# Cross-attention and mixture-of-experts block: the start-up ("filling") of the attention pipeline rearranged

## The chip, the core and the metric

The kernel runs on one core of a Trainium2 chip. The metric is the device time of one execution in microseconds (us); lower is better. The engines are TensorE (PE in the profile, its weight loads PEld), VectorE (DVE), ScalarE (ACT), GpSimd (POOL) and SyncE (SP, which here only issues transfers). They run side by side and wait for each other on semaphores.

## The reference, cut to what matters

```python
# x (2,1024,256), ctx (2,154,256); 16 heads of 16; 8 experts, 2 chosen per token, hidden 1024
def attention(query, ctx):                        # _L0_xattn_ref
    q = einsum('bsd,hdk->bhsk', query, Wq) + bq   # queries
    k = einsum('bsd,hdk->bhsk', ctx, Wk) + bk     # keys
    v = einsum('bsd,hdk->bhsk', ctx, Wv) + bv     # values, with their bias
    attn = softmax(einsum('bhqk,bhsk->bhqs', q, k) / sqrt(16))
    return concat_heads(attn @ v) @ Wo + bo
x = x + attention(layernorm(x), ctx)
x = x + experts(layernorm(x))                     # router, top 2 of 8, gelu MLP, weighted sum
```

## The kernel before, in words

The 2048 tokens are worked on in 8 pairs of tiles (m = 0 to 7, 256 tokens each; four pairs per batch entry). For each pair the kernel normalises x (`norm1`), turns it (`xn_transposes`), makes the queries (`q_product`, evacuated by `evac_q`) and splits them into a high and a low part (`evac_q` on ScalarE, `low_queries` on GpSimd), so that fp32 accuracy comes out of fast products. The two parts must then be spread over partitions into the tile `QS` (rows 0 to 31 high, 32 to 63 low, 64 to 95 high again, 96 to 99 the negated maxima). For pair 0 the engines copy them there on chip (`first_queries` on ScalarE, line 707, the loop at line 948 on VectorE, `first_low_queries` on GpSimd, line 519). For all other pairs SP stores them to the DRAM tensor `qd` (`queries`, line 376), and GpSimd's queue reads them back into `QS` (`queries_read`, lines 505 and 506). `by_memory(m)` says how many such round trips the slot of pair m has seen; the ring has four slots.

With `QS` and the keys `KS`, `scores(m, n)` (line 1477, n = 0 to 7) makes the scores of a pair into one of two buffers of PSUM, VectorE takes their maxima (`maxima`, line 1001), negates and splits them (`negatives`), TensorE turns them (`maxima_transposes`, line 1492), ScalarE evacuates them (`evac_maxima`, line 675), SP stores them and GpSimd's queue reads them into rows 96 to 99 of `QS` (`maxima_read`, line 511). Then `turned_scores(m, n)` (lines 1523 and 1526, n = 0 to 9) makes the scores again, keys on partitions, less the maxima; ScalarE takes their exponentials (`exp`, line 684), and `value_sums` (lines 1549 and 1551) multiplies them by the values.

The order on each engine is written out by hand; each engine carries out its list strictly in that order. First stands a filling, in which pairs 0 and 1 pass their scores; then step m (0 to 7) interleaves `scores` of pair m+2, `turned_scores` of pair m, and `value_sums` and the output projection of pair m-1. Step 0 begins with `scores(2, 0)`. After the attention come the routing and the expert products (lines 1826, 1843, 1846), where TensorE is busy nearly all the time.

The values are made once, in the filling: `value_product(b)` (lines 1451 and 1455) for b = 0 and 1, one after the other, before `scores(0, 0)`. VectorE adds the bias while it places them (`values`, lines 981 and 987) and writes the column of ones (`all_values`, line 993); both stand in VectorE's list between pair 0's and pair 1's maxima. In the same stretch ScalarE's list has `ones` (line 713, the selector rows of `KS`), `last_keys` (line 726), `evac_q`, `evac_xnT` and `evac_maxima`. TensorE's list there is: `value_product(0)`, `value_product(1)`, `scores(0, 0..7)` with pair 2's transposes and query product among them, `maxima_transposes(0)`, `scores(1, 0..7)` with pair 3's, `maxima_transposes(1)`, and then step 0.

Of the kernel before, what the change touches and what calls it, by code (L numbers as in the profile page):

```python
# [7 lines left out]
B, S, D = 2, 1024, 256  # L8
# [26 lines left out]
def xattn_moe_kernel(nc, x, ctxT, wq, bq, wk, bk, wv, bv, wo, bo, rwT, wexp,  # L35
# [11 lines left out]
    with ExitStack() as ctx:  # L47
# [196 lines left out]
        q0_high, q0_mid, q0_low = sem("q0_high"), sem("q0_mid"), sem("q0_low")  # L244
        ld_x2, ld_id, ld_bq = sem("ld_x2"), sem("ld_id"), sem("ld_bq")
        v_psum, v_made = sem("v_psum"), sem("v_made")
# [44 lines left out]
        def by_memory(m):  # L291

            return m // RING + int(m % RING > 0)
# [58 lines left out]
        def _(sp):  # L352
# [46 lines left out]
            queries(1)  # L399
# [30 lines left out]
        def _(pool):  # L430
# [51 lines left out]
            def low_queries(m):  # L482
                u = m % 2
                pool.wait_ge(q_hi_made, m + 1)
                if m >= 3:
                    pool.wait_ge(qd_stored[(m - 2) % RING], 64 * by_memory(m - 2))
                pool.tensor_tensor(Q2[:, u, 1, :, :].bitcast(f32r), qf[:, :, :], Q2[:, u, 0, :, :],
                                   ALU.subtract).then_inc(q_lo_made, 1)
# [24 lines left out]
            def first_low_queries():  # L513

                low_queries(0)
                for r in range(4):
                    pool.wait_ge(*((q0_low, r) if r else (q_lo_made, 1)))
                    pool.tensor_copy(QS[32:64, 0, 2 * r:2 * r + 2, :], Q2[32 * r:32 * r + 32, 0, 1, :, :]).then_inc(q0_low, 1)
                pool.wait_ge(q0_low, 4)  # L520
# [111 lines left out]
        def _(act):  # L632
# [23 lines left out]
            def evac_q(m):  # L656
                act.wait_ge(q_psum, m + 1)
                if m >= 1:
                    act.wait_ge(q_lo_made, m)
                for g in range(GROUPS):  # L660
# [3 lines left out]
                if m == 2:  # L664
                    act.wait_ge(q0_low, 4)
                if m >= 3:
# [37 lines left out]
            def first_queries():  # L704

                for r in range(4):
                    act.activation(QS[0:32, 0, 2 * r:2 * r + 2, :], qf[32 * r:32 * r + 32, :, :], ACT.Copy).then_inc(q0_high, 1)
# [30 lines left out]
            first_queries()  # L738
# [171 lines left out]
        def _(dve):  # L910
# [66 lines left out]

            def values(b):
                dve.wait_ge(v_psum, b + 1)
                bank = ps_v[b]  # L980
                dve.tensor_tensor(V_main[:, b, :, 0:DK], bank[:, 0:D].rearrange("p (h c) -> p h c", h=HEADS),
                                  bv_sb[:, :].rearrange("p (h c) -> p h c", h=HEADS), ALU.add).then_inc(v_made, 1)
                for j in range(4):
                    lanes = slice(32 * j, 32 * j + REM)
                    rest = bank[lanes, D:2 * D].rearrange("p (q j c) -> p q j c", j=4, c=DK)
                    bvr = bv_sb[lanes, :].rearrange("p (q j c) -> p q j c", j=4, c=DK)
                    dve.tensor_tensor(V_rest[lanes, b, :, 32 * j:32 * j + DK], rest[:, :, j, :], bvr[:, :, j, :],
                                      ALU.add).then_inc(v_made, 1)
            def all_values():
                dve.wait_ge(ld_v, 32)  # L990
                dve.wait_ge(v_zeroed, 2)
                for j in range(4):
                    dve.memset(V_rest[32 * j:32 * j + REM, :, :, 32 * j + DK:32 * j + DK + 1], 1.0).then_inc(v_made, 1)
                for b in range(B):
                    values(b)
# [64 lines left out]
            all_values()  # L1060
# [352 lines left out]
        def _(pe):  # L1413
# [35 lines left out]
            def value_product(b):  # L1449
                for c in range(KC):  # L1450
                    mm(ps_v[b][:, 0:D], ctx_sb[:, c, b * KEYS:b * KEYS + P], wv_sb[:, c, :],
                       start=c == 0, stop=c == KC - 1)
                for c in range(KC):
                    for j in range(4):
                        last = mm(ps_v[b][32 * j:32 * j + REM, D:2 * D],
                                  ctx_sb[:, c, b * KEYS + P:(b + 1) * KEYS], wv_sb[:, c, :],
                                  start=c == 0, stop=c == KC - 1)
                last.then_inc(v_psum, 1)

            def scores(m, n):  # L1460

                i, k, u, b = n // 4, n % 4, m % RING, m // (MACROS // B)
                if n == 0:
                    if by_memory(m):
                        pe.wait_ge(qs_loaded[u], 32 * by_memory(m))
                    else:
                        for made in (q0_high, q0_mid, q0_low):
                            pe.wait_ge(made, 4)
                        pe.wait_ge(k_made, 2)
# [29 lines left out]
            def turned_scores(m, n):  # L1499
# [5 lines left out]
                if n == 0:  # L1505
# [3 lines left out]
                    if m == 0:  # L1509
                        pe.wait_ge(v_made, 4 + 5 * B)  # L1510
# [137 lines left out]
            for b in range(B):  # L1648
                value_product(b)
# [78 lines left out]
            def step(m, has):  # L1728
                if m >= QUIET:
                    quiet_step(m)  # L1730
                    return
                if has(2):
# [7 lines left out]
                if has(0):  # L1740
# [12 lines left out]
                if has(0):  # L1753
                    turned_scores(m, 1)
# [162 lines left out]
```

## Time and profile before

| | us |
|---|---|
| Runs of the kernel before | 454.33, 457.53, 464.33 (median 457.53) |
| The profiled execution's own time | 454.56 |
| Its span | 452.6 |
| TensorE busy in the span | 397.0 (88%) |
| VectorE, ScalarE, GpSimd busy | 275.9, 228.6, 201.6 |
| Mean granted TensorE clock | 0.95 of full |

The profile is one execution. Its time is the span and 1.96 us around it. Starts are counted from the start of the span. A line of the timeline merges instructions of one kind that follow each other, so its length can hold short waits, and neighbouring matmul lines overlap by the pipeline. The granted clock is 1.00 (2.4 GHz) or 0.50 (1.2 GHz); a value between is a stretch with both.

### The profile page before, as it was taken

How to read it: one execution, taken by the hardware profiler on the slowest of the kernel's cores; microseconds unless marked ns; L12 is line 12 of the kernel's file. 1: busy time of each engine (PE TensorE's matmuls, PEld its weight loads, DVE VectorE, ACT ScalarE, POOL GpSimd, SP SyncE). 2: the span in 40 equal slices, each digit the busy share in tenths (PEclk: the TensorE clock that was granted, in tenths of full speed). 3: DMA queues.
4: the chain of work that ended last, by engine and by line, in shares of the span. 5: the costliest groups of instructions: out<-in, count | busy, mean ns of one | idle time of the engine just before them, and what ended most of it. 6: DMA issues, size and time to landing. Idle time of an engine off the chain costs nothing.

```text
span 452.6 us, 8677 instructions
## 1 busy us (share of the span) xinstructions
PE 397.0 (88%) x2742; PEld 332.7 (74%) x2743; DVE 275.9 (61%) x655; ACT 228.6 (51%) x420; POOL 201.6 (45%) x183
## 2 busy tenths in 40 slices
PE   6766798999999998658899999999999999999920
PEld 3445666768667675626899999999999999999910
DVE  2989748456476757787857556454466867464300
ACT  1843647456455654332674655544567766544300
POOL 4947567372623322005153644535445544452230
PEclk9986998999999999859999999999999999999985
DMA  7455552433610111754636435343252662332220
GB/s 240 133 116 123 122 121 76 97 98 73 169 42 13 54 49 47 234 187 126 247 68 180 82 105 143 58 129 47 47 139 47 220 151 38 55 49 25 25 28 12
DMA packets 25750, 45.39 MB, mean 100 GB/s; under 512 B 6512, under 2 KB 19952, under 8 KB 22960
## 3 DMA queue, kind: packets, MB, share of 16 engines
q0 software_dynamic: 8448, 15.77, 19.4%
q1 hardware_dynamic: 13760, 26.32, 18.2%
q10 hardware_dynamic: 3504, 2.83, 2.1%
q8 instruction: 20, 0.33, 0.3%
q14 instruction: 18, 0.15, 0.1%
HBM read 31.52 MB, written 13.39 MB: 99 GB/s over the span
## 4 chain that ended last, share of the span: by engine, by line
PE 73%; DVE 11%; DMA 4%; issue 3%; ACT 2%; POOL 1%; SPq 0%; ACTq 0%; DVEq 0%; POOLq 0%
PE ps_s L1826 23%; PE ps_t L1843 15%; PE ps_t L1846 8%; PE ps_s L1477 3%; DVE mx L1001 2%; PE ps_t L1526 2%; PE ps_a L1551 2%; PE ps_a L1549 2%; DMA result<-big,rowtok 2%; PE ps_c L1551 2%; PE ps_c L1808 2%; PE ps_t L1523 2%; PE ps_c L1549 2%; PE ps_t L1420 2%; PE ps_a L1577 1%
## 5 line engine op out<-in xcount | busy, mean ns | idle before, releaser
L1826 PE MATMUL ps_s<-xgT,KB 128*128 128x256 f32 x912 | 115.4, 282 | 3.0 <-DVE xgT L1358 3.0
L622 POOL DMA_INDIRECT result<-big,rowtok x38 | 66.8, 1759 | 112.3 <-DMA result<-big,rowtok 54.8
L1826 PEld LDWEIGHTS ps_s<-xgT,KB 128*128 128x128 f32 x912 | 110.1, 189 | 4.1 <-DVE xgT L1358 1.7
L1001 DVE TENSOR_REDUCE mx<-ps_s 128x4 f32<-128x616 f32 x64 | 49.3, 797 | 31.1 <-PE ps_s L1477 31.0
L590 POOL DMA_INDIRECT big<-rows,gtok x38 | 43.3, 1140 | 31.9 <-DVE gtok L1315 14.7
L1843 PE MATMUL ps_t<-KB,HTb 128*128 x160 | 56.0, 392 | 0.0
L684 ACT ACTIVATE big<-ps_t 128x512 f32<-128x512 f32 x80 | 45.2, 593 | 20.7 <-PE ps_t L1526 18.0
L876 ACT ACTIVATE big<-ps_t,wrow 128x256 f32<-128x256 f32 x38 | 18.0, 474 | 70.1 <-PE ps_t L1846 70.1
L1843 PE MATMUL ps_t<-KB 128*128 x144 | 50.4, 392 | 0.0
L1404 DVE SCALAR_TENSOR_TENSOR big<-ps_t,wrow,big 128x256 f32<-128x256 f32 x38 | 18.4, 483 | 52.5 <-ACT big L876 49.2
L868 ACT ACTIVATE big<-ps_s 128x512 f32<-128x512 f32 x76 | 45.5, 599 | 0.0
L1846 PE MATMUL ps_t<-KB,HTb 128*128 x160 | 44.7, 280 | 0.0
L1477 PE MATMUL ps_s<-KB 96*128 96x308 f32 x128 | 33.7, 357 | 7.6 <-DVE mx L1001 3.6
L1846 PE MATMUL ps_t<-KB 128*128 x144 | 40.3, 280 | 0.0
L452 POOL TENSOR_TENSOR mv<-mv,half_sb 128x2 f32<-128x2 f32 x15 | 10.9, 728 | 59.7 <-DVE mv L1045 42.6
L1843 PEld LDWEIGHTS ps_t<-KB,HTb 128*128 128x128 f32 x160 | 30.0, 188 | 6.3
L1374 DVE TENSOR_TENSOR KB<-big,KB 128x512 fp32r<-128x512 f32 x36 | 24.4, 691 | 16.1 <-ACT big L868 16.1
L866 ACT ACTIVATE HTb<-ps_s 128x512 fp32r<-128x512 f32 x40 | 24.0, 600 | 20.1 <-PE ps_s L1826 17.6
L1374 DVE TENSOR_TENSOR HTb<-big,HTb 128x512 fp32r<-128x512 f32 x40 | 26.6, 689 | 11.0 <-ACT big L868 11.0
L1526 PE MATMUL ps_t<-KB 100*128 100x256 f32 x128 | 29.3, 325 | 4.2 <-ACT big L684 3.9
L1477 PEld LDWEIGHTS ps_s<-KB 96*128 96x128 f32 x128 | 21.4, 208 | 13.7 <-DVE mx L1001 6.9
L1843 PEld LDWEIGHTS ps_t<-KB 128*128 128x128 f32 x144 | 27.0, 187 | 5.6
(234 smaller groups left out, 710.3 us busy)
## 6 DMA issues: line engine op xcount, KB each, us to landing
VP<-in_wexp SPq DMA_DIRECT2D x8, 1024.0 KB, 5.3
big<-in_wexp SPq DMA_DIRECT2D x8, 1024.0 KB, 5.5
qd<-big SPq DMA_DIRECT2D x28, 128.0 KB, 2.3
KB<-qd POOLq DMA_DIRECT2D x7, 512.0 KB, 5.3
result<-x SPq DMA_DIRECT2D x8, 256.0 KB, 2.7
rows<-xn SPq DMA_DIRECT2D x8, 256.0 KB, 2.9
KB<-qd POOLq DMA_DIRECT2D x7, 256.0 KB, 6.0
XS<-in_x ACTq DMA_DIRECT2D x1, 1024.0 KB, 5.8
```

What stands on the lines that cost most here:

```text
L590: pool.indirect_dma_start(XG[:, n, :], None, rows, bass.IndirectOffsetOnAxis(gtok[:, n:n + 1], 0)).then_inc(xg_loaded[u % 2], 16)
L622: pool.indirect_dma_start(out, bass.IndirectOffsetOnAxis(rowtok[:, u, h:h + 1], 0), ys[:, 2 * (u % 2) + h, :], None, compute_op=ALU.add).t ...
L684: act.activation(dst, ps_t[(n + 1) % 2][:, :].rearrange("p (h n) -> p h n", h=2), ACT.Exp).then_inc(p_made, 1)
L866: act.activation(hidT[u % 2][:, 0, 2 * b:2 * b + 2, :], ps_s[b // 2][:, b % 2, :].rearrange("p (j n) -> p j n", j=2), ACT.Gelu)
L868: act.activation(hid[:, b, :], ps_s[b // 2][:, b % 2, :], ACT.Gelu).then_inc(hid_made, 1)
L1001: dve.tensor_reduce(mx[:, i, :, 2 * k:2 * k + 2].rearrange("p a b -> p b a"), ps_s[n % 2][:, :, 0:2 * KEYS].rearrange("p b (h k) -> p b h ...
L1374: dve.tensor_tensor(hidT[u % 2][:, 1, js, :], hid[:, b, :].rearrange("p (j n) -> p j n", j=2), hidT[u % 2][:, 0, js, :].bitcast(fp32), ALU ...
L1477: last = mm(ps_s[n % 2][:, j, 0:2 * KEYS], QS[0:96, u, p, i * P:(i + 1) * P], KS[0:96, b, p, :], start=True, stop=True)
L1526: last = mm(bank[:, h, :], KS[0:100, b, place(j - 2), h * KEYS:h * KEYS + P], QS[0:100, u, place(j - 2), :], start=True, stop=True)
L1826: last = mm(ps_s[j // 4][:, j // 2 % 2, (j % 2) * PAIR:(j % 2 + 1) * PAIR], w1[:, w, k, j * P:(j + 1) * P], xgT[:, u % 2, a, k, :], start= ...
L1843: mm(ps_t[h][:, :].rearrange("p (w d) -> p w d", w=2), hidT[u % 2][:, 0, j, half_rows], w2[:, bass.ds(par, 1), :, j, :].squeeze(1), start= ...
L1846: last = mm(ps_t[h][:, 0:D], hidT[u % 2][:, 1, j, half_rows], w2[:, bass.ds(par, 1), 0, j, :].squeeze(1), start=False, stop=j == HJ - 1, s ...
```

## The change

Four things are changed, all in the filling and at the head of step 0.

1. The bias of the values is added by TensorE: one more product (identity by the bias rows) for each main and each remainder group. ScalarE copies the result into place. VectorE keeps only the four small writes of ones, now before its copies of pair 0's queries.
2. Pair 1's queries are no longer stored and read back. ScalarE copies the high part twice (`first_queries(1)`, `queries_again`), GpSimd the low part (`first_low_queries(1)`). The counts of round trips change with it.
3. `value_product(1)` stands behind `scores(0, 7)`, ahead of `maxima_transposes(0)`. On ScalarE, `ones(0)` now stands whole behind `evac_q(2)`, `last_keys(0)` behind `evac_maxima(0)`, and then both `values`. GpSimd's queue takes `maxima_read(0)` ahead of `queries_read(2)`.
4. In step 0 `turned_scores(0, 0)` and `(0, 1)` stand first, ahead of `scores(2, 0)`.

```diff
         def by_memory(m):
-            return m // RING + int(m % RING > 0)
+            return m // RING + int(m % RING > 1)
@@ sync
-            queries(1)
             queries(2)
             maxima(0)
@@ gpsimd
             def low_queries(m):
-                if m >= 3:
+                if m >= 4:
                     pool.wait_ge(qd_stored[(m - 2) % RING], 64 * by_memory(m - 2))
-            first_low_queries()
+            first_low_queries(0)
             middle_keys(0)
-            low_queries(1)
-            queries_read(1)
+            first_low_queries(1)
             low_queries(2)
             next_norm1(3)
+            maxima_read(0)
             queries_read(2)
-            maxima_read(0)
             next_norm1(4)
@@ scalar
+            def queries_again():
+                for r in range(4):
+                    act.activation(QS[64:96, 1, 2 * r:2 * r + 2, :], qf[32 * r:32 * r + 32, :, :], ACT.Copy).then_inc(q1_mid, 1)
+
+            def values(b):
+                act.wait_ge(v_psum, b + 1)
+                act.wait_ge(v_zeroed, 2)
+                bank = ps_v[b]
+                act.activation(V_main[:, b, :, 0:DK], bank[:, 0:D].rearrange("p (h c) -> p h c", h=HEADS),
+                               ACT.Copy).then_inc(v_made, 1)
+                for j in range(4):
+                    lanes = slice(32 * j, 32 * j + REM)
+                    rest = bank[lanes, D:2 * D].rearrange("p (q j c) -> p q j c", j=4, c=DK)
+                    act.activation(V_rest[lanes, b, :, 32 * j:32 * j + DK], rest[:, :, j, :], ACT.Copy).then_inc(v_made, 1)
...
-            first_queries()
+            first_queries(0)
...
             evac_q(1)
-            ones(0, (0,))
+            first_queries(1)
             evac_xnT(2)
-            ones(0, (1,))
+            queries_again()
+            evac_q(2)
+            ones(0)
+            evac_maxima(0)
             last_keys(0)
-            evac_q(2)
-            evac_maxima(0)
+            values(0)
+            values(1)
             evac_xnT(3)
@@ vector
+            dve.wait_ge(v_zeroed, 2)
+            for j in range(4):
+                dve.memset(V_rest[32 * j:32 * j + REM, :, :, 32 * j + DK:32 * j + DK + 1], 1.0).then_inc(v_ones, 1)
             dve.wait_ge(qf_made, 1)
...
             statistics1(3)
-            all_values()
@@ tensor, value_product(b)
+                mm(ps_v[b][:, 0:D], id_sb[:, :], bv_sb[:, :], start=False, stop=True)
...
+                for j in range(4):
+                    last = mm(ps_v[b][32 * j:32 * j + REM, D:2 * D], id_sb[:, 32 * j:32 * j + REM], bv_sb[:, :],
+                              start=False, stop=True)
@@ tensor, filling
-            for b in range(B):
-                value_product(b)
+            value_product(0)
...
             for n in range(4 + GROUPS, 8):
                 scores(0, n)
+            value_product(1)
             maxima_transposes(0)
@@ tensor, step(m, has)
+                if m == 0:
+                    turned_scores(0, 0)
+                    turned_scores(0, 1)
                 if has(2):
                     scores(m + 2, 0)
```

The waits are changed to match: `scores(1, 0)` waits for the copies instead of the read, and `turned_scores(0, 0)` for ten placed values and the four writes of ones.

## Rows read from the trace of the kernel before

**Rows 1.** Busy time by stage: PE, PEld, DVE, ACT, POOL, granted clock, DMA.

```profile
330.00:370.00 40.00, 40.00 (x286) 37.52 (x286) 27.84 (x56) 25.09 (x45) 19.00 (x15) 1.00 0.55 151
```

**Rows 2.** The chain that ended last, 43 to 60 us: start, length, what.

```profile
43.83 0.88 PE ps_c L1444 x4
...
48.98 2.22 DMA qd<-big
...
52.13 5.66 DMA KB<-qd
...
57.83 0.55 PE ps_s L1477 x2
```

**Rows 3.** TensorE's timeline of the filling: start, length, line, operation.

```profile
18.15 1.03 PE L1451 MATMUL ps_t<-big 128*128 128x256 f32 x4
...
20.10 1.13 PE L1451 MATMUL ps_t<-big 128*128 128x256 f32 x4
...
31.12 0.55 PE L1477 MATMUL ps_s<-KB 96*128 96x308 f32 x2 [0.60 <-DVE mx L1001]
33.20 0.40 PE L1492 MATMUL ps_a<-id_sb,nm 128*32 128x128 f32 x2 [1.53 <-DVE nm L1014]
35.47 1.40 PE L1477 MATMUL ps_s<-KB 96*128 96x308 f32 x4 [1.88 <-DMA KB<-qd]
...
45.16 0.40 PE L1492 MATMUL ps_a<-id_sb,nm 128*32 128x128 f32 x2 [0.47 <-DVE nm L1014]
45.31 0.82 PE L1477 MATMUL ps_s<-KB 96*128 96x308 f32 x4
45.97 0.65 PE L1523 MATMUL ps_t<-KB 100*128 100x256 f32 x4
...
51.48 1.89 PE L1444 MATMUL ps_c<-xnT,wq_sb 128*128 128x256 f32 x8
...
57.03 0.38 PE L1492 MATMUL ps_c<-id_sb,nm 128*32 128x128 f32 x2
```

**Rows 4.** VectorE's timeline of the filling.

```profile
22.98 2.03 DVE L1054 TENSOR_SCALAR xn<-XS,mv 128x256 f32<-128x256 f32 x2
...
34.17 0.47 DVE L993 MEMSET VP<- 26x8 f32 x4
...
37.34 1.51 DVE L1001 TENSOR_REDUCE mx<-ps_s 128x4 f32<-128x616 f32 x2
...
45.89 2.25 DVE L1001 TENSOR_REDUCE mx<-ps_s 128x4 f32<-128x616 f32 x3 [0.78 <-PE ps_s L1477]
```

**Rows 5.** ScalarE's timeline of the filling.

```profile
13.00 2.57 ACT L707 ACTIVATE KB<-qf 32x512 fp32r<-32x512 f32 x4
...
28.18 0.84 ACT L726 ACTIVATE KB<-KB 100x104 fp32r<-100x104 f32 x4
29.98 0.84 ACT L661 ACTIVATE qf<-ps_a,bq_sb 128x256 f32<-128x256 f32 x2 [0.97 <-PE ps_a L1444]
...
41.29 2.34 ACT L713 ACTIVATE KB<-own 4x1232 fp32r<-4x1232 f32 x2
```

**Rows 6.** GpSimd's timeline of the filling.

```profile
17.07 2.87 POOL L519 CAST KB<-big 32x512 fp32r<-32x512 f32 x4
...
23.59 1.27 POOL L487 TENSOR_TENSOR big<-qf,big 128x512 fp32r<-128x512 f32 x1
...
35.13 2.44 POOL L463 TENSOR_SCALAR xn<-XS,mv 128x256 f32<-128x256 f32 x2
...
38.22 0.53 POOL L506 DMA_DIRECT2D KB<-qd  x1
```

**Rows 7.** Stages at low granted clock, columns as in the first group.

```profile
24.60:28.20 3.60, 3.13 (x11) 2.79 (x12) 3.29 (x5) 1.84 (x3) 0.26 (x1) 0.55 0.54 135
...
35.10:42.00 6.90, 5.21 (x18) 4.46 (x19) 6.32 (x19) 1.31 (x2) 4.19 (x6) 0.51 0.72 159
76.10:79.40 3.30, 3.28 (x15) 1.73 (x16) 1.72 (x6) 0.80 (x2) 2.16 (x3) 0.51 0.68 199
```

More of the change, by code:

```diff
@@ L511, in maxima_read, with first_low_queries @@
                 pool.dma_start(QS[96:100, u, :, :], md[u, :, :].rearrange("(r q) n -> r q n", q=PAIRED)).then_inc(nm_loaded[u], 16)
-            def first_low_queries():
-                low_queries(0)
+            def first_low_queries(m):
+                low_queries(m)
                 for r in range(4):
-                    pool.wait_ge(*((q0_low, r) if r else (q_lo_made, 1)))
-                    pool.tensor_copy(QS[32:64, 0, 2 * r:2 * r + 2, :], Q2[32 * r:32 * r + 32, 0, 1, :, :]).then_inc(q0_low, 1)
-                pool.wait_ge(q0_low, 4)
+                    pool.wait_ge(*((q0_low, 4 * m + r) if r else (q_lo_made, m + 1)))
+                    pool.tensor_copy(QS[32:64, m, 2 * r:2 * r + 2, :], Q2[32 * r:32 * r + 32, m, 1, :, :]).then_inc(q0_low, 1)
+                pool.wait_ge(q0_low, 4 * m + 4)
             def middle_keys(b):
@@ L659, in evac_q @@
                     act.wait_ge(q_lo_made, m)
+                if m == 2:
+                    act.wait_ge(q0_high, 8)
+                    act.wait_ge(q1_mid, 4)
                 for g in range(GROUPS):
@@ L663, in evac_q @@
                 last.then_inc(qf_made, 1)
-                if m == 2:
-                    act.wait_ge(q0_low, 4)
-                if m >= 3:
+                if m in (2, 3):
+                    act.wait_ge(q0_low, 4 * m - 4)
+                if m >= 4:
                     act.wait_ge(qd_stored[(m - 2) % RING], 64 * by_memory(m - 2))
@@ L976, in low_keys @@
                                     KM[b][32 * r:32 * r + 32, 1, :, :, :].rearrange("p g a k -> p (g a k)")).then_inc(ks_low, 1)
[L978 to L993, printed above, removed]
-                for b in range(B):
-                    values(b)
             def maxima(m, n):
@@ L1451, in value_product @@
                     mm(ps_v[b][:, 0:D], ctx_sb[:, c, b * KEYS:b * KEYS + P], wv_sb[:, c, :],
-                       start=c == 0, stop=c == KC - 1)
+                       start=c == 0, stop=False)
+                mm(ps_v[b][:, 0:D], id_sb[:, :], bv_sb[:, :], start=False, stop=True)
                 for c in range(KC):
                     for j in range(4):
-                        last = mm(ps_v[b][32 * j:32 * j + REM, D:2 * D],
-                                  ctx_sb[:, c, b * KEYS + P:(b + 1) * KEYS], wv_sb[:, c, :],
-                                  start=c == 0, stop=c == KC - 1)
+                        mm(ps_v[b][32 * j:32 * j + REM, D:2 * D],
+                           ctx_sb[:, c, b * KEYS + P:(b + 1) * KEYS], wv_sb[:, c, :],
+                           start=c == 0, stop=False)
+                for j in range(4):
+                    last = mm(ps_v[b][32 * j:32 * j + REM, D:2 * D], id_sb[:, 32 * j:32 * j + REM], bv_sb[:, :],
+                              start=False, stop=True)
                 last.then_inc(v_psum, 1)
@@ L1466, in scores @@
                     else:
-                        for made in (q0_high, q0_mid, q0_low):
-                            pe.wait_ge(made, 4)
-                        pe.wait_ge(k_made, 2)
+                        for made in (q0_high, q0_low):
+                            pe.wait_ge(made, 4 * m + 4)
+                        pe.wait_ge((q0_mid, q1_mid)[m], 4)
+                        if m == 0:
+                            pe.wait_ge(k_made, 2)
                     if m % (MACROS // B) == 0:
@@ L1509, in turned_scores @@
                     if m == 0:
-                        pe.wait_ge(v_made, 4 + 5 * B)
+                        pe.wait_ge(v_made, 5 * B)
+                        pe.wait_ge(v_ones, 4)
                     if m >= 1:
@@ L1647, in _ @@
             pe.wait_ge(ld_v, 32)
-            for b in range(B):
-                value_product(b)
+            value_product(0)
             for n in range(2):
@@ L1731, in step @@
                     return
+                if m == 0:
+                    turned_scores(0, 0)
+                    turned_scores(0, 1)
                 if has(2):
@@ L1739, in step @@
                     value_sums(m - 1, 1)
-                if has(0):
+                if has(0) and m:
                     turned_scores(m, 0)
@@ L1753, in step @@
                 if has(0):
-                    turned_scores(m, 1)
+                    if m:
+                        turned_scores(m, 1)
                     turned_scores(m, 2)
```

8 lines of the change are left out of this document (4 added, 4 removed).

## The prediction

> **What bounds the kernel now.** I read the busy time by stage first: from the expert stage on TensorE is busy for all of a 40 us window [rows 1], and nothing of the change is there. What the filling gains or loses can therefore only arrive as a shift of everything behind it. So I read the chain of waits next, to see what sets the start of step 1, the first stretch in which TensorE's list runs without waits. It is pair 3's queries: from the second half of their product at 43.83 by way of ScalarE, GpSimd, SP's four stores (the last lands 2.22 later) and the read back (5.66) to `scores(3, 0)` at 57.83, 14.0 in all [rows 2]. But that chain wins narrowly. TensorE's own list ends step 0 with `maxima_transposes(2)` at 57.03 [rows 3]; the same pair of lines follows at 0.15 distance elsewhere (45.16, 45.31, rows 3), so without the read `scores(3, 0)` would start at 57.2. A faster chain alone is worth 57.83 - 57.2 = 0.6; more has to come from an earlier step 0. There VectorE's maxima set the pace: they start at 45.89 [rows 4], and pair 4's query product waits behind them until 51.48 [rows 3].
>
> **The change part by part.** I walk the lists with the durations of the trace; a small "+" is against before.
>
> *Start, VectorE.* The four writes of ones take 0.47 to 0.50 with the gaps [rows 4]. They stood between pair 0's and pair 1's maxima and now stand ahead of a stretch in which VectorE never rests, so pair 2's normalised x, finished at 25.01 [rows 4], comes 0.5 later. Its transposes and product follow. Part of their work moves past 28.2, where the granted clock rises from half (0.55 on average until then, rows 7) to full, so I count +0.4 from there on. `ks_low` also comes 0.5 later (23.45) and stays just inside GpSimd's copies; `scores(0, 0)` does not move.
>
> *Pair 1's queries.* ScalarE: four copies take 2.57 [rows 5], twice. The first set ends at 22.8 + 2.6 = 25.4, before pair 2's transposes at 26.7; the second ends at 29.9, before pair 2's product at 30.4. Nobody waits for ScalarE. GpSimd: `low_queries(1)` ends at 24.86 and the copies take 2.87 [rows 6], to 27.7; its next work needs pair 2's queries at 31.9. So all of pair 1 is in place by 29.9, where the read let `scores(1, 0)` start at 35.47 [rows 3]. SP loses four stores, GpSimd's queue two reads.
>
> *Values on TensorE.* One `value_product` takes 20.10 - 18.15 = 1.95 [rows 3]. The bias is one more product for each two, so 2.9 with it. `value_product(0)` ends at 21.2 instead of two at 22.2: hidden, `scores(0, 0)` waits until 23.76 for keys. `value_product(1)` now starts behind `scores(0, 7)`, 31.67 [rows 3] + 0.4 less overlap = 32.0, ends at 34.9, and holds back `maxima_transposes(0)`, which was at 33.20 [rows 3]: +1.7. Behind it `scores(1, 0)` starts at 35.1 against 35.47: the read that is saved is nearly all spent on this product.
>
> *VectorE freed.* Before, `maxima(1, 0)` waited for VectorE, which was placing values until 37.34 [rows 4]. Now VectorE takes it 0.55 behind the scores, at 35.65. Four maxima (3.0), `statistics1(4)` (1.2), four maxima (3.0) follow, to 42.7; before to 44.67. Negatives and a hand-over are 0.5: `maxima_transposes(1)` at 43.2 against 45.16 [rows 3], -2.0.
>
> *Values on ScalarE.* `evac_maxima(0)` at 35.3 to 35.7; `last_keys` 0.84 [rows 5]; then ten placements. None is in the trace on ScalarE. By the nearest rows a wide one is 128x256, 0.42 (half of 0.84), a small one between 0.2 and 0.28 (a 100x104 copy, both rows 5): 1.2 to 1.5 for each b; I take 1.25 because the small ones are 64 columns. All end at 39.05, then `evac_xnT(3)` to 39.7 (turned by 38.5, so this is now 0.5 to 0.6 late), `ones(1)` 2.34 [rows 5] to 42.0. TensorE makes the two halves of pair 3's product at 39.75 and, behind `scores(1, 7)`, at 41.7 to 42.6. The head of the chain at 43.83 becomes 41.7, and its end 57.79 becomes 55.6: -2.2. GpSimd is not in its way: `norm1(4)` ends at 43.1, ScalarE delivers at 44.15.
>
> *GpSimd's queue.* GpSimd ends `norm1(3)` (2.44, rows 6) at 38.0; the maxima are stored by 35.75 + 2.0 = 37.75. `maxima_read(0)` costs 0.53 of issue ahead of `queries_read(2)`, whose second read then goes out at 39.2 instead of 38.22 [rows 6] and lands 5.66 later [rows 2] at 44.9. Before, it was there at 43.9 and held nobody; now `scores(2, 0)` waits for it. The two turned scores put ahead (0.65 and 0.3, rows 3) fit into 43.4 to 44.7, so they cost nothing here, and are cover for the read. The maxima are there by 43.7 at the latest. `scores(2, 0)` at 44.9 against 45.31, -0.4; VectorE's maxima follow with the same -0.4, and with them pair 4's product, its queries and the last five exponentials.
>
> *Step 1.* TensorE: 57.2 - 0.4 = 56.8. The read: 55.6, no longer late. `scores(3, 0)` at 56.8 instead of 57.83.
>
> **The sum:** -1.0. Of the 2.2 that the chain gains, 1.2 are not used, since step 0's own list is next in line. The profiled execution took 454.56, so 453.5. Its own time lies 3 us under the median of the three runs (457.53) and at their lowest, which I take up in the range.
>
> **One cover that may be thin.** Pair 2's second normalisation is slow: both take 2.03 [rows 4], while GpSimd's subtraction runs beside it [rows 6]. Behind that subtraction now stand four copies of 0.72 where GpSimd was idle. If one of them gets in first, pair 2 comes another 0.7 later, the read's landing moves from 44.9 to 45.6, step 1 to 57.5, and the gain shrinks to 0.3: 454.2. The Trainium skill ("SBUF — State Buffer", "Who interferes with whom") says that a VectorE instruction in a two-port mode and a GpSimd one exclude each other for the whole instruction, and that order of issue decides. The slow row agrees; by this rule one or two such losses are to be expected, and the sum would be 454.2 instead of 453.5. I keep 453.5, because the two normalisations now start before the copies do.
>
> **The rivals.**
> *Slower: `value_product(1)` at half clock.* The granted clock came back at 28.2 after a stretch in which TensorE was busy 3.13 of 3.60 [rows 7]. The stretch now starts 0.5 later after a longer pause (from 21.2, not 22.2). If it comes back only with the next busy stretch, pair 2's product and the scores beside it lose about 1.5, and the product of 2.9 can cost 5.8. Then `maxima_transposes(0)` stands at 34.9 + 1.5 + 2.9 = 39.3, its maxima are stored at 42.1, `queries_read(2)` lands at 49.0, VectorE starts at 49.6, 3.7 late, and step 1 at 60.9: 457.7. It decides from the point where `maxima_transposes(0)` starts later than 36.3 (from there the read lands so late that step 1 is back at 57.8). For it: the lower clock did hit 6.9 us in a row from 35.1 [rows 7]. Against it: from 25.6 on work is dense. With half clock for the scores only it gives 454.7. Chance 0.2.
> *More gain: the whole chain.* If the read lands with time to spare (there are two reads less on the queue, and the maxima go first) and step 0 shortens too, all of 2.2 is gained: 452.4. Against it: the reads took the same time alone, and turned scores hold TensorE until 44.7, so -0.6 is the most that step 0 can give by this list. Chance 0.05.
> *The dip moves.* From 76.1 to 79.4 TensorE was granted half clock while busy for 3.28 [rows 7]; half of that, 1.6, is lost. The clock does not follow my shift exactly; the dip may vanish (451.9) or a second one come (455.1). The half clock from 35.1 to 42.0 should go, since `value_product(1)` fills the pause before it, but VectorE sets the pace there. Chance 0.15.
> *The change doesn't do what it says*: the values placed by ScalarE turn out so slow (over 0.6 for a small one) that pair 3's transposes wait and the chain is back at 57.8: 454.6 or a little more. Chance 0.05.
>
> **How the numbers follow.** The forecast (453 to 454.6 with the thin cover inside) has 0.55. The likeliest time is 453.5. The low end is the vanished dip with the largest gain, 452.4 - 1.6, rounded to 450.5. The high end is the half-clock rival, 457.7, with the distance of about 1.5 by which a median may lie over a single execution: 459. A difference of 2% (9.1 us) is about what a measurement of this kernel can tell from no change; no case comes near it on either side. Only the spread of the runs (454.33 to 464.33) could bring it about: faster 0.03, slower 0.03, within 0.94.
>
> **What would show it.** In the profile after: `value_product(1)` between 32.0 and 34.9; the first maxima of pair 1 at 35.7 instead of 37.34; ScalarE's ten placements in 2.5; no wait for a read before `scores(3, 0)`, but one before `scores(2, 0)`, near 44.9; the granted clock full from 35 to 42; step 1 at 56.8. It would be wrong if `maxima_transposes(0)` starts after 36.3, if `scores(2, 0)` comes later than 45.9, or if `scores(3, 0)` still ends a wait for its read.

## The result and the profile after

The changed kernel takes 458.98 us (median of 20 runs, 454.43 to 467.0), the kernel before 455.36 (20 runs, 452.25 to 464.33). Their ratio is 1.0064, with a 95% interval of 1.0039 to 1.0089: 0.64% or 2.9 us slower, where 1.0 less was forecast. The ratio leaves out runs more than 1.5% above the fastest of their kernel, so it is not that of the two medians; the execution that was profiled, 461.63, is such a run, and I therefore read from its trace where time went, and take no size from its total.

Two rows of the page of the changed kernel, the span and the granted clock in 40 slices:

```profile
span 459.8 us, 8726 instructions
...
PEclk9889799999999999669999999999999998999975
```

**The filling did nearly what was forecast up to 47 us.** TensorE's timeline of the changed kernel (start, length, line, operation, wait ahead of it); it answers to [rows 3]:

```profile
32.23 1.03 PE L1454 MATMUL ps_t<-big 128*128 128x256 f32 x4
...
34.50 0.61 PE L1464 MATMUL ps_t<-bv_sb,id_sb 128*26 128x256 f32 x8
35.05 0.39 PE L1502 MATMUL ps_a<-id_sb,nm 128*32 128x128 f32 x2
35.20 0.82 PE L1487 MATMUL ps_s<-KB 96*128 96x308 f32 x4
...
43.26 0.39 PE L1502 MATMUL ps_a<-id_sb,nm 128*32 128x128 f32 x2 [0.58 <-DVE nm L1018]
...
45.50 0.83 PE L1487 MATMUL ps_s<-KB 96*128 96x308 f32 x4 [1.05 <-DMA KB<-qd]
...
52.03 2.92 PE L1447 MATMUL ps_c<-xnT,wq_sb 128*128 128x256 f32 x8
...
58.62 0.38 PE L1502 MATMUL ps_c<-id_sb,nm 128*32 128x128 f32 x2
58.76 0.53 PE L1487 MATMUL ps_s<-KB 96*128 96x308 f32 x2
```

`value_product(1)` stands behind `scores(0, 7)`, `scores(1, 0)` waits for no read, the second turned maxima come 1.9 earlier than before (43.26 against 45.16), and a read is now waited for at `scores(2, 0)`. Then pair 4's query product takes 2.92 instead of 1.89 [rows 3], and step 1 starts at 58.76, 0.93 later than before.

The other engines of the changed kernel, VectorE's timeline (it answers to [rows 4]), ScalarE's [rows 5] and GpSimd's [rows 6]:

```profile
22.95 2.03 DVE L1058 TENSOR_SCALAR xn<-XS,mv 128x256 f32<-128x256 f32 x2
...
35.77 2.96 DVE L1005 TENSOR_REDUCE mx<-ps_s 128x4 f32<-128x616 f32 x4 [0.74 <-PE ps_s L1487]
```

```profile
36.61 0.36 ACT L719 ACTIVATE VP<-ps_t 128x256 f32<-128x256 f32 x1
36.88 0.92 ACT L724 ACTIVATE VP<-ps_t 26x64 f32<-26x64 f32 x4
37.82 0.38 ACT L719 ACTIVATE VP<-ps_t 128x256 f32<-128x256 f32 x1
38.10 0.92 ACT L724 ACTIVATE VP<-ps_t 26x64 f32<-26x64 f32 x4
```

```profile
24.89 2.61 POOL L518 CAST KB<-big 32x512 fp32r<-32x512 f32 x4
...
35.89 2.43 POOL L462 TENSOR_SCALAR xn<-XS,mv 128x256 f32<-128x256 f32 x2
38.60 0.81 POOL L510 DMA_DIRECT2D KB<-md  x1 [0.27 <-DMA md<-nmT]
```

The clock took back what was won. Busy time by stage of the changed kernel, columns as in [rows 1], and the expert stage's window under it:

```profile
35.00:47.00 12.00, 8.24 (x47) 5.75 (x43) 8.27 (x18) 8.96 (x24) 9.50 (x10) 1.00 0.51 117
47.00:55.00 8.00, 7.92 (x30) 7.04 (x31) 6.86 (x15) 2.29 (x5) 5.29 (x7) 0.57 0.74 160
...
76.00:79.40 3.40, 3.08 (x26) 1.40 (x25) 2.20 (x8) 1.69 (x4) 1.69 (x2) 1.00 0.69 189
330.00:370.00 40.00, 40.00 (x283) 37.38 (x282) 29.19 (x58) 25.86 (x46) 18.33 (x12) 1.00 0.52 144
```

The half clock of 35.1 to 42.0 and that of 76.1 to 79.4 [rows 7] are gone; a new stretch at 0.57 lies at 47 to 55, where TensorE is busy for 7.92 of 8.

**The time was lost in the expert stage.** Its first product starts at 209.61 before and at 208.49 after, 1.1 earlier; TensorE's last product ends at 432.66 and 440.96, 8.3 later. The expert stage grew from 223.05 to 232.47. Two pauses of TensorE, 2.52 and 4.88, are 7.4 of these 9.4, both for the rows that GpSimd gathers for one of the later experts; before has no such pause. Most of the rest is a stretch of 3.4 at half clock that begins at 378.4, as the second pause ends. TensorE's timeline, first the kernel before, then the changed one:

```profile
276.74 2.04 PE L1826 MATMUL ps_s<-xgT,KB 128*128 128x256 f32 x16
278.61 0.60 PE L1808 MATMUL ps_c<-id_sb,big 128*128 128x128 f32 x4
```

```profile
280.27 0.66 PE L1823 MATMUL ps_c<-id_sb,big 128*128 128x128 f32 x4 [2.52 <-DMA big<-rows,gtok]
...
378.68 1.12 PE L1823 MATMUL ps_c<-id_sb,big 128*128 128x128 f32 x4 [4.88 <-DMA big<-rows,gtok]
```

The window of [rows 1] lies between the two: it is as full as before, and shows nothing.

### The profile page after: what moved, and what is told of

The parts are those of the page before. It is cut to its first block, busy times and chain, and to the rows that moved or that the text cites. A ratio compares the mean times of both kernels' runs of the same rounds, so it can differ in the third digit from the quotient of the medians.

```text
span 459.8 us, 8726 instructions
## 1 busy us (share of the span) xinstructions
PE 402.5 (88%) x2762; PEld 336.7 (73%) x2763; DVE 274.0 (60%) x645; ACT 235.5 (51%) x438; POOL 208.0 (45%) x185
## 4 chain that ended last, share of the span: by engine, by line
PE 59%; DMA 12%; DVE 11%; issue 5%; ACT 4%; POOL 2%; DVEq 0%; ACTq 0%; POOLq 0%
PE ps_s L1841 17%; PE ps_t L1858 10%; DMA result<-big,rowtok 7%; PE ps_t L1861 5%; PE ps_s L1487 3%; PE ps_t L1537 3%; DMA big<-rows,gtok 3%; DVE mx L1005 2%; PE ps_a L1562 2%; PE ps_c L1562 2%; PE ps_a L1560 2%; PE ps_t L1534 2%; PE ps_c L1560 2%; PE ps_c L1823 1%; PE ps_t L1423 1%
## 5 line engine op out<-in xcount | busy, mean ns | idle before, releaser
L620 POOL DMA_INDIRECT result<-big,rowtok x38 | 69.9, 1840 | 115.7 <-DMA result<-big,rowtok 70.8
L588 POOL DMA_INDIRECT big<-rows,gtok x38 | 45.2, 1190 | 31.7 <-DVE gtok L1318 14.9
L1407 DVE SCALAR_TENSOR_TENSOR big<-ps_t,wrow,big 128x256 f32<-128x256 f32 x38 | 18.4, 483 | 55.0 <-ACT big L896 54.5
L1858 PEld LDWEIGHTS ps_t<-KB,HTb 128*128 128x128 f32 x160 | 30.0, 188 | 6.3
L1861 PEld LDWEIGHTS ps_t<-KB,HTb 128*128 128x128 f32 x160 | 30.1, 188 | 0.0
```

The source lines that it names most:

```text
L588: pool.indirect_dma_start(XG[:, n, :], None, rows, bass.IndirectOffsetOnAxis(gtok[:, n:n + 1], 0)).then_inc(xg_loaded[u % 2], 16)
L620: pool.indirect_dma_start(out, bass.IndirectOffsetOnAxis(rowtok[:, u, h:h + 1], 0), ys[:, 2 * (u % 2) + h, :], None, compute_op=ALU.add).t ...
L1858: mm(ps_t[h][:, :].rearrange("p (w d) -> p w d", w=2), hidT[u % 2][:, 0, j, half_rows], w2[:, bass.ds(par, 1), :, j, :].squeeze(1), start= ...
L1861: last = mm(ps_t[h][:, 0:D], hidT[u % 2][:, 1, j, half_rows], w2[:, bass.ds(par, 1), 0, j, :].squeeze(1), start=False, stop=j == HJ - 1, s ...
```

## The experiments

All intervals are 95% intervals of the ratio to the kernel before. The expert stage is measured in each trace from its first product to TensorE's last.

The expectations name their theories by letters. A: the loss sits in the expert stage, carried by GpSimd's queue of gathers and adds. B: it sits in the filling. Later, I: the position of TensorE's instructions in its list makes the pause. R: rounding of the values sends tokens to other experts.

**Which part does it?** Three kernels undo one part each, and the changed kernel runs again beside them.

Turned scores back behind `scores(2, ...)`:

```diff
-                if m == 0:
-                    turned_scores(0, 0)
-                    turned_scores(0, 1)
...
-                if has(0) and m:
+                if has(0):
...
-                    if m:
-                        turned_scores(m, 1)
+                    turned_scores(m, 1)
```

> The changed kernel with part 4 undone: scores(2, 0) again first in step 0, turned_scores(0, 0) and (0, 1) in their old places. Theory B (late read, then half clock in step 0): the turned scores no longer fill the wait, so step 0 is longer by up to 1 and the first expert product moves to 209 or later. Theory A: the attention may move by less than 1 and the total stays near 1.006 of before, since no transfer changes.

Measured: 0.9986 (0.9919 to 1.0053); expert stage 225.99, with a pause of 2.43.

Pair 1's queries by memory again (the waits and `by_memory` are changed back with it):

```diff
+            queries(1)
             queries(2)
...
-            first_low_queries(1)
+            low_queries(1)
+            queries_read(1)
...
-            first_queries(1)
             evac_xnT(2)
-            queries_again()
```

> The changed kernel with part 2 undone: pair 1's queries go by memory again (four stores, two reads on GpSimd's queue), with the other parts in place. Theory A, with GpSimd's queue as the carrier: the number of transfers that this queue has taken before the expert stage is that of before again, so the expert stage is back near 223 and the total near 1.000, though the attention is later by 1 to 3, as value_product(1) now delays pair 1 and the read is late too. Theory B: the filling is slower still, total 1.01 or more.

Measured: 1.0043 (1.0001 to 1.0085); expert stage 225.95, with a pause of 2.73. Neither theory's forecast for the trace came: the queue's transfers are those of before again, yet the pause is there, so their number is not the cause; and the filling is not slower in the trace, where the first expert product comes at 206.96, earlier than in any other here.

Bias and placing of the values back on VectorE, both value products first (the small products for the bias are gone from TensorE):

```diff
-            value_product(0)
+            for b in range(B):
+                value_product(b)
...
-            value_product(1)
...
             statistics1(3)
+            all_values()
...
-            values(0)
-            values(1)
```

> The changed kernel with parts 1 and 3's place of value_product(1) undone: VectorE adds the bias and places the values, both products stand before scores(0, 0); pair 1's queries copied on chip and the turned scores first stay. By the walk of the prediction maxima_transposes(0) is back at 33.2, scores(1, 0) follows at once, but VectorE is busy with the values until 37.3 as before: the attention within 1 of before. Theory A: total still near 1.005, since the queue's transfers are those of the changed kernel. Theory B: the half clock in step 0 goes, total 0.997 to 1.000.

Measured: 1.0016 (0.9983 to 1.0049); expert stage 223.12, no pause, though the queue's transfers are those of the changed kernel.

The changed kernel again:

> The changed kernel, unchanged, for a second profile and a second comparison. In the first profile the attention was ahead (the first expert product at 208.5 against 209.6) and the expert stage longer (from that product to TensorE's end 232.5 against 223.1, with two waits for gathered rows of 2.5 and 4.9). Theory A, the loss sits in the expert stage, where GpSimd's one queue carries gathers and adds: first expert product again near 208.5, expert stage at least 225, ratio near 1.006. Theory B, the loss sits in the filling (the read of pair 2's queries comes late and TensorE drops to half clock in step 0) and the first profile was a lucky one there: first expert product at 211 or later, expert stage near 223.

Measured: 0.9991 (0.9955 to 1.0026); expert stage 225.79, with a pause of 2.50 at 276.9. The first expert product comes at 207.66, not at 211 or later, so B's forecast failed. A's stage came, its ratio near 1.006 did not. Of the two pauses the first came back, in `u_turned` and `u_queries` too; the second, 4.88, did not. Only the kernel whose values stay on VectorE is without it. Two reasons remain. The one, routing: the values' bias is rounded otherwise when TensorE adds it, so tokens could go to other experts. The other, position: the ten bias products in 32-bit floats are forty instructions (each is two products and two weight loads in the trace), with the waits that the change adds some 42; the whole list of TensorE behind them moves by as much.

**Position or routing?** The kernel before, with 21 tiny products (42 instructions) put in at its start:

```diff
             keep_busy(17)
+            for _ in range(21):
+                mm(ps_t[0][:, 0:32], ones_bf[:, :], ones_bf[:, 0:32], start=True, stop=True)
```

> The kernel before with 21 products of 32 columns behind the warming ones at the start, in a pause of TensorE: 42 more instructions of TensorE, as many as the change adds (20 matmuls, 20 weight loads, 2 waits), and nothing else changed. Theory I: the instruction packet moves from 54.5 to 52.5, between the packets of the adds, the wait of 2.5 comes, the expert stage is 225.8, ratio 1.005 to 1.007. Theory R (the bias added in another place rounds the values otherwise, and other tokens go to the experts): values are those of before, so expert stage 223.1, ratio 1.000.

Measured: 1.0029 (0.9984 to 1.0074); expert stage 225.84, with a pause of 2.51 at 282.2. Nothing of the change is in it, its values are those of before, and the pause is there. The ratio is under the 1.005 to 1.007 that was expected.

The same 21 products in the changed kernel:

> The changed kernel with the same 21 small products. Theory I: the instruction packet moves on by another 2 to 3, to about 50, where no packets of gathers or adds are; the expert stage is back near 223 and the total is the gain of the attention alone, ratio 0.996 to 0.998. Theory R: nothing moves, expert stage 225.8, ratio as the changed kernel.

Measured: 1.0002 (0.996 to 1.0044); expert stage 224.73, a pause of 1.13. A miss for theory I: the pause is shorter but not gone, and the packet did not move on to 50; it lies at 53.0, where the changed kernel without the 21 products has it too (52.7 to 52.9).

The changed kernel with 40 instructions less: the runs of empty products that are meant to keep the clock up (`keep_busy`), at the start and ahead of the expert stage, are made of fewer and longer ones.

```diff
+            def keep_busy_fp32(n):
+                for _ in range(n):
+                    mm(ps_t[0][:, :].rearrange("p (a n) -> p a n", a=4), zero[:, 0:P],
+                       zero[:, 0:P].unsqueeze(1).to_broadcast([P, 4, P]), start=True, stop=True)
...
-            keep_busy(17)
+            pe.wait_ge(zero_made, 1)
+            keep_busy_fp32(4)
...
-            keep_busy(20)
+            keep_busy_fp32(4)
+            keep_busy(1)
```

> The changed kernel with its 37 warming products of bf16 (512 columns) replaced by 8 of fp32 on a tile of zeros and 1 of bf16, about as long together, with 40 instructions fewer: TensorE's instruction count ahead of the expert stage is that of before plus a few. Theory I: the packet is back at 54.5, the expert stage 223.1, the total 0.996 to 0.998 of before. Theory R: expert stage 225.8.

Measured: 0.9988 (0.9948 to 1.0027); expert stage 223.25, no pause, with the values of the change. Routing is refuted from both sides: a pause with the old values, none with the new.

The kernel before again:

> The kernel before, unchanged, for its second profile. So far every trace with the values' bias on TensorE (four of four) has a wait of 2.4 to 2.7 for gathered rows 69 us into the expert stage, and neither of the two with the values on VectorE has it (the kernel before, u_values). Theory I (position of TensorE's instructions): no such wait here, expert stage 223.1 from the first expert product to TensorE's end, one 16 KB packet of the instruction queue between 54.5 and 55 us into it, ratio 1.000. If it were chance: the wait can be here too, near 226.

Measured: 1.0027 (0.9992 to 1.0062); expert stage 223.08, no pause. A kernel against itself gives 1.0027: single comparisons differ by that much.

One of them comes 52.5 to 54.5 us after the first expert product. DMA by queue, in windows of 2 us at the same place behind that product (52 to 54, and 54 to 56 where a second follows); columns: packets, MB, share of 16 engines. Before, changed kernel, before with 21 products, changed kernel with 40 instructions less:

```profile
q0 software_dynamic: 210, 0.33, 72.0%
q1 hardware_dynamic: 38, 0.18, 21.8%
...
q0 software_dynamic: 30, 0.07, 9.4%
q8 instruction: 1, 0.02, 2.9%
```

```profile
q0 software_dynamic: 205, 0.33, 68.1%
q1 hardware_dynamic: 38, 0.18, 22.5%
q8 instruction: 1, 0.02, 2.9%
```

```profile
q0 software_dynamic: 196, 0.31, 66.9%
q1 hardware_dynamic: 45, 0.24, 29.2%
q8 instruction: 1, 0.02, 2.9%
```

```profile
q0 software_dynamic: 204, 0.32, 68.2%
q1 hardware_dynamic: 46, 0.25, 29.6%
...
q0 software_dynamic: 36, 0.07, 10.3%
q8 instruction: 1, 0.02, 2.9%
```

In the second and third the packet lies among the dense packets of queue 0, GpSimd's gathers and its add; in the first and last it comes when these are nearly through. Its place goes with the count, but not in step. 16 products and as many weight loads take 2.04 in the expert stage (276.74, above), so 42 instructions are, as an estimate, 2.7 us of TensorE's list; from before to `b_pad21` the packet moves by 1.7 (54.6 to 52.9), from the changed kernel to `a_pad21` not at all, though the next one there moves from 69.4 to 65.5. The Trainium skill ("Runtime: NRT & Kernel Launch", "Instruction fetch mechanics") says that an engine's list is fetched in blocks of 16 KiB, and that crossing a block is mostly hidden. The 16 KB packets agree. Whether TensorE itself waits for a block no run here tests; if the reading below is right, this one had a cost all the same, by way of the gathers. What follows is in GpSimd's timeline, same order of kernels:

```profile
264.63 1.63 POOL L622 DMA_INDIRECT result<-big,rowtok  x1 [2.70 <-DMA result<-big,rowtok]
...
271.54 1.02 POOL L590 DMA_INDIRECT big<-rows,gtok  x1 [0.30 <-issue]
272.86 1.19 POOL L590 DMA_INDIRECT big<-rows,gtok  x1 [0.30 <-issue]
```

```profile
264.29 1.63 POOL L620 DMA_INDIRECT result<-big,rowtok  x1 [3.38 <-DMA result<-big,rowtok]
...
272.76 1.46 POOL L588 DMA_INDIRECT big<-rows,gtok  x1 [0.30 <-issue]
```

```profile
268.76 1.63 POOL L622 DMA_INDIRECT result<-big,rowtok  x1 [3.42 <-DMA result<-big,rowtok]
...
277.22 1.46 POOL L590 DMA_INDIRECT big<-rows,gtok  x1 [0.31 <-issue]
```

```profile
264.54 1.63 POOL L620 DMA_INDIRECT result<-big,rowtok  x1 [2.46 <-DMA result<-big,rowtok]
...
272.38 1.23 POOL L588 DMA_INDIRECT big<-rows,gtok  x1 [0.30 <-issue]
```

The add ahead of these gathers waits 3.4 for an earlier one to land, instead of 2.5 to 2.7. So the next two gathers are issued 0.7 and 1.0 later after the first expert product, and the second one ends its issue behind an issue of SP that it otherwise beats, the 1 MB load of the next expert's weights. SP's own list, before and changed kernel:

```profile
274.43 0.33 SPq L392 DMA_DIRECT2D VP<-in_wexp  x1
```

```profile
273.40 0.33 SPq L392 DMA_DIRECT2D VP<-in_wexp  x1
```

Before, the second gather ends at 272.86 + 1.19 = 274.05, ahead of 274.43; changed, at 272.76 + 1.46 = 274.22, behind 273.40. Its rows then land too late, and TensorE waits 2.5. The order holds in all 18 traces of this text: the nine without a pause have the gather's end ahead of the load, the nine with one behind it. Where the landing is on record, the gather lands 3.0 to 3.1 after its start without the pause (5 traces) and 7.4 to 7.7 after it with it (3). Two things stay open. No kernel here moves the load alone. And `a_pad21` has the long wait of the add (3.43) and the turned order, but a pause of 1.13 only; its next instruction packet lies at 65.5 instead of 69.4, which may be the reason and was not tested.

**Is it repeatable, and what is the change worth without it?** The changed kernel and the one with 40 instructions less again, and two further edits on the latter. First the repeats:

> The changed kernel a third time, beside the same with 40 instructions fewer (next). Theory I (position of TensorE's instructions): expert stage 225.8 or more with the wait of 2.5 near 69 us into it, instruction packet at 52.5; from the end of pair 2's normalisation to the first expert product 183.4 (182.5 to 184.6 in the four traces with this order); ratio 1.003 (attention -1.2, expert stage +2.7). Theory R (rounding) expects the same here.

Measured: 1.0009 (0.9963 to 1.0054); expert stage 227.16, with a pause of 2.48 and, as it ends, a stretch of 3.4 at half clock.

> The changed kernel with the 37 warming products replaced by 9, 40 instructions fewer, a second time. Theory I: expert stage 223.2, packet at 54.5, ratio 0.997, and 2 to 3 us below a_third in the same job. Theory R: as a_third.

Measured: 0.9977 (0.9945 to 1.0009); expert stage 223.10, no pause.

Pair 2's queries read ahead of the maxima, on the shortened kernel (the changed kernel with 40 instructions less):

```diff
-            maxima_read(0)
             queries_read(2)
+            maxima_read(0)
```

> The version with 40 instructions fewer, and GpSimd's queue takes queries_read(2) ahead of maxima_read(0) as before the change. By the walk the read of pair 2's queries then lands 0.7 to 0.9 earlier (44.7 instead of 45.5 in the trace after), scores(2, 0) no longer waits 1.05 but at most 0.3, and the maxima land by 44.5 and may hold turned_scores(0, 0) by up to 1. If the late read is what costs step 0 its time: attention 0.5 to 0.8 shorter, ratio 0.996. If the one transfer only swaps places with the other: attention as a_short2.

Measured: 1.0003 (0.9965 to 1.004). A miss: TensorE now waits 1.75 at 44.8 for the maxima, and later 1.71 and 1.15, as its timeline shows:

```profile
46.59 0.74 PE L1539 MATMUL ps_t<-KB 100*128 100x256 f32 x4 [1.75 <-DMA KB<-md]
...
55.33 0.88 PE L1492 MATMUL ps_s<-KB 96*128 96x308 f32 x2 [1.71 <-DVE mx L1005]
```

Nothing here speaks for the old order of the two reads.

Both value products first, on the shortened kernel:

```diff
-            value_product(0)
+            for b in range(B):
+                value_product(b)
...
-            value_product(1)
```

> The version with 40 instructions fewer, and value_product(1) again directly behind value_product(0). By the walk scores(0, 0) starts 0.4 later (the two products end at 24.1), maxima_transposes(0) at 33.9 and scores(1, 0) at 34.1 instead of 35.1, so pair 1's maxima are 1.0 earlier, and the maxima of pair 0 are stored 1.0 earlier, though GpSimd's norm1(3) sets when they are read: attention 0.3 to 0.8 shorter. Against it: TensorE has a pause between 32.2 and 33.9 again, and half clock may follow it as in the kernel before (35.1 to 42.0); VectorE sets the pace there, so it costs at most 0.5.

Measured: 0.9963 (0.9927 to 0.9999); expert stage 223.09, no pause.

Then each of the four main kernels once more:

> The kernel before with 21 small products at the start, again. Theory I (position of TensorE's instructions): packet at 52.5, expert stage 225.8, ratio 1.004 to 1.007. If the packet's place costs only in some executions, the trace can have it and the ratio is within 0.003 of 1.

Measured: 1.0031 (0.9997 to 1.0065), again under what was expected; expert stage 227.45, pause 2.61, and half clock for 3.4 as it ends.

> The changed kernel, a fourth time. Theory I: packet at 52.5, expert stage 225.8 or more, ratio 1.001 to 1.005 (the three so far: 1.0064, 0.9991, 1.0009), above a_short3 by 0.004 to 0.006.

Measured: 0.9978 (0.9927 to 1.0028); expert stage 226.00, pause 2.71.

> The changed kernel with 40 instructions fewer ahead of the expert stage, a third time. Theory I: packet at 54.5, expert stage 223.1 to 223.3, ratio 0.997 to 0.999 (so far 0.9988, 0.9977).

Measured: 0.996 (0.9928 to 0.9993); expert stage 223.05, no pause.

> The same with value_product(1) again directly behind value_product(0), a second time. The first gave 0.9963 (0.9927 to 0.9999), its trace an attention no shorter than that of a_short2 (183.6 from the end of pair 2's normalisation to the first expert product in both) and an expert stage of 223.1. If the place of value_product(1) gains something, ratio below 0.998 again; if not, it is that of a_short3 within 0.003.

Measured: 0.9972 (0.9934 to 1.001); expert stage 223.21, no pause.

**Taken together.** 18 traces fall into groups by where the instruction packet lies behind the first expert product (read in steps of 0.5 us):

| packet at | kernels | traces | expert stage | pause |
|---|---|---|---|---|
| 53.5 to 54.5 | before twice, `u_values`, `a_short` three times, `s_reads`, `s_vfirst` twice | 9 | 223.05 to 223.25 | none |
| 53.0 | `a_pad21` | 1 | 224.73 | 1.13 |
| 52.5 | changed four times, `u_turned`, `u_queries`, `b_pad21` twice | 8 | 225.79 to 232.47 | 2.43 to 2.73 |

So with the packet at 52.5 the pause costs 2.7 in the trace (225.8 - 223.1), whatever else is in the kernel, and 4.1 and 4.4 in the two traces where half clock follows it (227.16 and 227.45).

In times it is harder to see. Four comparisons of the changed kernel gave 1.0064, 0.9991, 1.0009 and 0.9978; they lie further apart than their intervals allow. Their plain mean is 1.0011, weighted by their intervals 1.0028. The shortened kernel's three (0.9988, 0.9977, 0.996) have means of 0.9975 and 0.9973. The shortening is thus worth 0.0036 to 0.0055, 1.6 to 2.5 us, not far from 2.7. The padded kernel before does not bear it out: it gave 1.0029 and 1.0031, where 2.7 us would be 1.006, and the kernel before, unchanged, gave 1.0027 beside it. So what the pause costs over many executions is not settled. That the changed kernel is slower than before by 2.9 holds for the first comparison; over all four it is 0.5 to 1.3 us slower, and the difference is not settled. The shortened changed kernel comes out 1.2 us faster than before (weighted 0.9973, half interval 0.0020). All three comparisons point that way, but one of a kernel with itself was off by as much (1.0027), so this is likely and not shown.

## Why the prediction was wrong

**The step that failed** is one of its first sentences: that nothing of the change is in the expert stage, so that the filling can only arrive as a shift. [rows 1] showed a stage in which TensorE is always busy, and it was still busy in that window after. But the list that TensorE reads there lies 42 instructions further on, and 2.7 us were lost at another place of the stage, most likely since a packet that fetches the list fell among GpSimd's gathers. I counted the bias products by their duration (about 0.95 of `value_product`'s 2.9) and not by their length in the list. `b_pad21` shows that the length alone brings the pause. The shift that was forecast, 1.0, did arrive (1.1); with 2.7 against it the trace would be 1.6 slower. The first comparison gave 2.9, the mean of four 0.5 to 1.3.

**The second pause** of the profiled execution (4.88 at 373.8) is in none of the seventeen other traces. It follows an add at 362.07 whose issue took 3.69 instead of 1.6. It is a cause of that execution's 461.63, and its own cause stays open.

**The filling, step by step.** Held: `value_product(1)` 32.23 to 35.1 (forecast 32.0 to 34.9); pair 1's maxima from 35.77 (35.65); the ten placements in 2.4 (2.5), a wide one 0.36, four small ones 0.92; `maxima_transposes(1)` at 43.26 (43.2); the wait moved from the read for `scores(3, 0)` to that for `scores(2, 0)`, at 45.50 (44.9); full clock from 35 to 42. Off by 0.5: pair 2's normalised x was to come 0.5 later and ended at 24.98 against 25.01, since the 0.47 of the writes were won back ahead of it (VectorE's four casts took 2.17 instead of 2.31, its masks 1.02 instead of 1.35). The thin cover was not tested: the rule of the Trainium skill ("SBUF — State Buffer", "Who interferes with whom") would have let GpSimd's copies delay that normalisation, but they started at 24.89, as it ended.

**Step 1 at 56.8** failed: 58.76. By 45.5 the list was 0.6 behind the forecast: GpSimd ended `norm1(3)` at 38.3, not 38.0, then waited 0.27 for the store of the maxima, and the issue of their read took 0.81, not 0.53. The rest is the half clock at 47 to 55. The rival of a dip that moves named this; it gave a dip no place in step 0. It was made good later: with the dip at 76.1 to 79.4 gone, step 2 ended 1.0 ahead of before (its last turned maxima at 95.27 against 96.23), and the expert stage began 1.1 ahead, which is the forecast's -1.0, by compensation and not by its steps. Over all traces the part from pair 2's normalised x to the first expert product takes 184.4 on average with the old placing of values (183.3 to 186.1, 5 traces) and 183.5 with the whole change (181.6 to 186.7, 8 traces); without the executions of more than 458 us it is 184.0 and 183.0 (4 and 6 traces). That is -0.9 or -1.0, less than the spread within either, so the forecast's gain is likely but not shown by this; the shortened kernel's -1.2 us points the same way. `u_queries`, where pair 1's queries go by memory, has 182.0, inside the range of the whole change: that this round trip is saved shows no gain by itself.

Two sums of the prediction are off by a little, without weight: VectorE's walk gives 42.85 and not 42.7, and the half-clock rival 457.6 and not 457.7.

**The order in the filling does not matter** where I thought it did. `s_vfirst` puts `value_product(1)` back ahead, and its attention part (183.6 and 185.1 in two traces) is no shorter than that of `a_short` (183.6 to 184.0 in three). The rival of `value_product(1)` at half clock was wrong in place: that product ran at full clock.

## What to carry to other kernels

Count what an edit adds to an engine's instruction list, not only how long it runs: the fetches of what stands behind it can move too. Where a late stage depends on gathers that only just arrive, read TensorE's waits over that whole stage after each change, not one window. And when a small change gives a surprise, put the same number of empty instructions into the old kernel; it costs one run and separates position from content. Then read its time as well as its trace: here the trace shows 2.7 us and the times do not.

## What the runs showed of the hardware

An instruction packet of 16 KB among the packets of a gather and an add goes with a longer wait for their landing: 3.21 to 3.43 in nine traces, 2.40 to 2.78 in the nine others. With it the order of two issues turned, and TensorE stopped for 2.4 to 2.7 (in one trace 1.1). Padding the kernel before with 42 instructions moved that packet by 1.7 us; the same padding of the changed kernel left it where it was.

In three of the eighteen traces half clock began within 0.7 us of the end of a pause for gathered rows and lasted 3.4 us (after the changed kernel's 4.88, `a_third`'s 2.48 and `b_pad21b`'s 2.61); behind the seven other pauses the clock stayed full.

The granted clock dips at other places in each execution of one program. The page's row of it for the changed kernel, run again (its first stands above), and for `s_vfirst`:

```profile
PEclk9988999999999999759999999999999999999975
```

```profile
PEclk9985989999999999858999999999999999999985
```

Over the first 100 us the mean granted clock was 0.93 in the kernel before and 0.91 in its repeat, 0.93, 0.97, 0.95 and 0.91 in the four traces of the changed kernel, and 0.98 in `u_queries`. The length of the attention part goes with the clock more than with the kernel. By the mean granted clock over that part, the eighteen traces have 181.6 to 183.6 us at 0.93 or 0.94 (7 traces, among them the padded kernel before), 183.3 to 184.6 at 0.92 (5, among them the kernel before twice), and 183.6 to 186.8 at 0.90 or 0.91 (6). A forecast below 1 us can't be tested by a single trace where a dip more or less is worth as much.
